# Second attention: queries laid out with tokens over partitions, normalized tile by tile and turned by DMA

## The reference

```python
q = (hidden_states @ q_proj_w.T).reshape(B, Q, NUM_HEADS, HEAD_DIM).transpose(0, 2, 1, 3)   # 32 heads of 128
k = (cross_attention_states @ k_proj_w.T).reshape(B, KV, NUM_KV_HEADS, HEAD_DIM).transpose(0, 2, 1, 3)  # 8 heads
v = ...
q = rmsnorm(q, q_norm_w)          # x * rsqrt(mean(x*x over the 128 of a head) + eps) * w
k = rmsnorm(repeat(k), k_norm_w)
scores = jnp.einsum('bhqd,bhkd->bhqk', q, k) * scale + attention_mask
attn = jax.nn.softmax(scores, axis=-1)
out = jnp.einsum('bhqk,bhkd->bhqd', attn, v)
return out.transpose(0, 2, 1, 3).reshape(B, Q, NUM_HEADS * HEAD_DIM) @ o_proj_w.T
```

## Time and profile before

| what | value |
|---|---|
| median of 3 runs | 2430.42 us (2430.31 to 2433.67) |
| profiled execution, its own time | 2431.65 us |
| its span, first to last instruction | 2429.8 us, granted TensorE clock 0.991 |
| PE busy | 2368.4 us, 97% |
| DVE, ACT, POOL busy | 67%, 52%, 50% |
| second attention, turns 0 to 30 | from 1395.67 us to 2346.45 us of the span |
| DMA, mean | 45 GB/s |

### The profile page before, as it was taken

One profiled execution on the slowest core, in us unless ns is written; L12 is line 12 of the kernel. 1 busy time (PEld: TensorE's weight loads), 2 busy tenths in 40 slices (PEclk: granted clock), 3 DMA queues, 4 the chain that ended last, 5 costly groups with the idle time before them and its releaser, 6 DMA issues.

```text
span 2429.8 us, 45008 instructions
## 1 busy us (share of the span) xinstructions
PE 2368.4 (97%) x17656; PEld 1296.2 (53%) x17664; DVE 1625.0 (67%) x3133; ACT 1253.3 (52%) x2425; POOL 1222.5 (50%) x981
## 2 busy tenths in 40 slices
PE   7899999999999999999999999999999999999998
PEld 4455555555555555444444655555555555555554
DVE  7877777767777788654443566667666666755666
ACT  7665655555555555423232555555555555544453
POOL 3556666666666666223331355444445555445531
PEclk9899999999999999999999999999999999999999
DMA  6111121212121121011100111122121212221101
GB/s 210 45 42 32 51 51 30 53 27 53 27 53 31 42 44 26 29 44 35 44 10 16 40 32 27 42 54 63 36 62 36 62 36 62 53 43 27 27 14 70
DMA packets 216753, 108.13 MB, mean 45 GB/s; under 512 B 169280, under 2 KB 192480, under 8 KB 216544
## 3 DMA queue, kind: packets, MB, share of 16 engines
q1 hardware_dynamic: 216544, 105.25, 17.5%
HBM read 61.62 MB, written 4.19 MB: 27 GB/s over the span
## 4 chain that ended last, share of the span: by engine, by line
PE 61%; POOL 14%; DVE 10%; issue 4%; ACT 4%; POOLq 0%; DVEq 0%; ACTq 0%
PE PB L859 16%; PE PB L811 14%; PE PB L971 9%; PE PB L795 6%; POOL AR L2690 5%; PE PB L988 5%; POOL AR L2695 4%; POOL PSP L2708 3%; PE PB L836 2%; PE PB L901 2%; DVE AR L2116 2%; DVE WB L1921 2%; PE PB L767 1%; POOL AR L2685 1%; ACT JUNK L1321 1%
## 5 line engine op out<-in xcount | busy, mean ns | idle before, releaser
L859 PE MATMUL PB<-WB,AR 128*128 128x512 f16 x3072 | 689.0, 381 | 8.2 <-issue 3.9
L811 PE MATMUL PB<-XTB,WB 128*128 128x512 f16 x3072 | 677.9, 379 | 3.4 <-ACT WB L1357 1.9
L859 PEld LDWEIGHTS PB<-WB,AR 128*128 128x128 f16 x3072 | 298.0, 98 | 368.0 <-issue 15.4
L811 PEld LDWEIGHTS PB<-XTB,WB 128*128 128x128 f16 x3072 | 297.0, 98 | 346.2 <-issue 3.1
L2701 POOL TENSOR_TENSOR AR<-AR,SML 128x512 f32<-128x512 f32 x128 | 144.6, 1151 | 317.0 <-DVE SML L2101 317.0
L2131 DVE SCALAR_TENSOR_TENSOR X<-PB,SML,X 128x512 f32<-128x512 f32 x256 | 189.4, 747 | 168.2 <-PE PB L859 162.0
L1481 ACT ACTIVATE AR<-PB 128x512 f16<-128x512 f32 x256 | 131.5, 596 | 233.1 <-PE PB L901 233.1
L2690 POOL TENSOR_TENSOR AR<-AR,CST 128x512 f32<-128x512 f32 x128 | 182.2, 1423 | 39.6 <-ACT AR L1391 39.6
L2011 DVE TENSOR_TENSOR AR<-PB,AR 128x512 f16<-128x512 f32 x128 | 88.1, 690 | 168.2 <-ACT AR L1444 168.2
L971 PE MATMUL PB<-XTB,AR 128*128 128x512 f16 (+1 forms) x864 | 192.5, 379 | 0.0
L1397 ACT ACTIVATE AR<-AR 128x512 f16<-128x512 f32 x128 | 80.5, 630 | 206.7 <-POOL AR L2695 205.3
(11 more groups left out here) (272 smaller groups left out, 3770.8 us busy)
## 6 DMA issues: line engine op xcount, KB each, us to landing
STG<-in_wo SPq DMA_DIRECT2D x14, 1024.0 KB
STG<-in_wq SPq DMA_DIRECT2D x13, 1024.0 KB
STG<-in_qw_gu SPq DMA_DIRECT2D x40, 128.0 KB
STG<-in_ctxT SPq DMA_DIRECT2D x4, 1024.0 KB
X<-in_x SPq DMA_DIRECT2D x4, 1024.0 KB, 11.1
out_x<-X SPq DMA_DIRECT2D x16, 256.0 KB, 2.4
STG<-in_wk SPq DMA_DIRECT2D x14, 256.0 KB
STG<-in_wv SPq DMA_DIRECT2D x14, 256.0 KB
```

The costliest lines, as they stand in the source:

```text
L811: m = pe.do.matmul(b[:, :], wq[x][:, k, h * 128:(h + 1) * 128], XT[y][c][:, k, :], start=n == 0, stop=n == 11)
L859: m = pe.do.matmul(b[:, :], AT[x][:, h, t * 128:(t + 1) * 128], wo[y][:, h, :], start=n == 0, stop=n == 11)
```

## The change

Only the second attention is touched.

- PE takes each 128-token tile t of the queries as the stationary operand and the weights of all four heads as the moving one: a bank now holds 128 tokens over partitions and 4 heads of 128 along it. There are as many matmuls, of the same size. `norm_q` and `turn_k` on PE are gone.
- For each tile: ACT squares (`squares_1`), DVE sums over each head's 128 and scales (`sums_1`, two instructions), POOL raises 4 columns to -1/2 (`power_1`), DVE multiplies the bank by them (`queries_1`), ACT writes the high half, POOL the low half (DVE for tile 3, `low_1`). The squares and sums of tile t stand ahead of the multiplication of tile t-1.
- SP turns two tiles, both halves, by two DMAs of 64 partitions each (`turn_q`), twice a unit. `scores` waits for the second (`qt_in`).
- Keys of units 0 and 1 are turned by DMA too. Keys and values of unit 2 are made at the end of turn 0 instead of in turn 1.
- In the softmax the multiplication by the norms is gone; the mask is added straight from PSUM.
- Output tiles use banks 4, 5, 2, 3 in turns up to the last but one.

```diff
+        QHP = [words(a, 1024, F16) for a in (10752, 5632)]
+        QHL = [QHP[t // 2][:, 1024 * (t % 2):1024 * (t % 2) + 1024] for t in range(4)]
+        QT_rows = words(0, 2048, F16).rearrange("p (o t n) -> p o t n", o=2, t=4)
...
+            return ((4, 5, 2, 3) if L and u < NU - 2 else (2, 3, 0, 2))[t]
...
+            def turn_q(u, two):
+                for t in (2 * two, 2 * two + 1):
+                    sp.wait_ge(q_hi, (1, u, t))
+                    sp.wait_ge(*halved(u, t))
...
+                for odd in range(2):
+                    sp.do.dma_start_transpose(out=QT_rows[:, odd, 2 * two:2 * two + 2, :].rearrange("p t (a q) -> p (t a) q", a=8),
+                                              in_=QHP[two][64 * odd:64 * odd + 64, :]).then_inc(qt_in.of((u, two), 16), 16)
...
+                    elif u < NU - 1:
+                        turn_p_pair(1, u, 0)
+                        turn_p_pair(1, u, 1)
+                        turn_q(u + 1, 0)
                         turn_k(u + 1)
+                        turn_q(u + 1, 1)
...
+            def queries_1(u, t):
...
+                        m = pe.do.matmul(b[:, :], XT[x][c][:, k, t * 128:(t + 1) * 128], wq[y][:, k, :],
+                                         start=n == 0, stop=n == 11)
...
+                if L:
                     pe.wait_ge(kt_in, u)
+                    pe.wait_ge(qt_in, (u, 1))
...
+                    if (L, u) == (1, 0):
+                        keys_values(2, 0)
+                        keys_values(2, 1)
...
+            def sums_1(u, t):
+                g, rs = UNITS[1][u][0], RSQ[:, 4 * t:4 * t + 4]
+                dve.wait_ge(q_sq, (u, t))
+                dve.do.tensor_reduce(rs, M1[t].rearrange("p (h d) -> p h d", h=4), AX, ALU.add).then_inc(q_sum.of((u, t)), 1)
+                dve.wait_ge(q_sum, (u, t))
+                dve.do.tensor_scalar(rs, rs, 1.0 / DH, eco(1, g, 0), ALU.mult, ALU.add).then_inc(q_ms.of((u, t)), 1)
+
+            def queries_1(u, t):
+                dve.wait_ge(q_pow, (u, t))
+                dve.do.tensor_tensor(M1[t].rearrange("p (h d) -> p h d", h=4), PB[QB[t]][:, :].rearrange("p (h d) -> p h d", h=4),
+                                     RSQ[:, 4 * t:4 * t + 4].unsqueeze(2).to_broadcast([128, 4, DH]), ALU.mult
+                                     ).then_inc(q_mul.of((u, t)), 1)
...
-                    dve.do.tensor_tensor(v[pair], by_batch(PB[4 + pair][:, :]),
-                                         RSQ[:, pair * BC:(pair + 1) * BC].unsqueeze(2).to_broadcast([128, BC, SQ]),
-                                         ALU.mult).then_inc(s_out.of((1, u, pair)), 1)
+                    dve.do.scalar_tensor_tensor(v[pair], by_batch(PB[4 + pair][:, :]), PWN[:, 2:3],
+                                                MASK1.unsqueeze(1).to_broadcast([128, BC, SQ]), ALU.mult, ALU.add
+                                                ).then_inc(s_out.of((1, u, pair)), 1)
...
+                    for t in range(4):
+                        power_1(u, t)
+                        if t > 0:
+                            queries_1(u, t - 1)
+                        if t < 2 and beside > 0:
+                            halved_p(1, beside, t)
+                        if t == 2 and u > 1:
+                            halved_k(u)
+                        side(1, beside, 1 + t)
```

361 lines of the change are left out of this document (170 added, 191 removed).

## The result

| | median of the runs, us | ratio to the kernel before, 95% interval | span, us | clock |
|---|---|---|---|---|
| before | 2430.36 | | 2429.8 | 0.991 |
| changed | 2523.56 (2521.29 to 2526.55) | 1.0381 [1.0369, 1.0393] | 2519.5 | 0.98 |

A forecast was written before the change was run, and what follows sets the result against it. PE, busy 97% of the span, was taken as the bound. From 2431.65 us, entry +9.7 and -0.6, later turns -5.6, -9.6, +2.5, -2.5 gave 2425.5; the runs' median, 1.2 lower, 2424.3; range 2404 to 2449.

The forecast's parts named there:

- PE's floor: PE, second attention: a turn without norm_q's 0.80 us takes 28.93; turns 12 to 15 together 116.5 instead of 118.9.
- Step 1: DVE's weighed, mask and maximum, then the softmax up to POOL's soft_norm: POOL starts at D + 8.41 us.
- D: Start of DVE's weighed, counted from the start of PE's scores: 0.68 us behind a turn with weight work.
- The entry: Turns 0 and 1: 65 us in place of 55.25, +9.7, through added PE idle time; -0.6 ahead of turn 0.
- nothing to 3.4 us for the clock: Turns 0 and 1: the clock behind the idle times costs between nothing and 3.4 us in each.
- step 4: SP issues two query transposes, 1.23 us to issue one, last landing 3.1 after its issue: D + 28.8.
- The rival with slow transposes: SP's last pair ahead of the scores: 2.5 us later, half of it per turn, kernel at 2448; 24%.
- steps 2 and 3: POOL without a gap to tile 3's power, 13.8 us, D + 22.2; then DVE, ACT, DVE to D + 24.3.
- a rival of its own: Path through DVE and POOL longer by 1 to 1.5 us: -0.2 a turn left, kernel at 2430; 24%.
- The loop forgives: PE waiting at scores lets DVE start weighed earlier: a path longer by x costs about x/2 a turn.
- only remove waits that PE doesn't have in plain turns: Output banks and sums-ahead order: worth nothing, covered by the 10.4 us of output tiles.
- 30 turns at -0.80: Rival: the wide cover holds everywhere, turns 0 and 1 come out even, kernel at 2405; 12%.

The follow-up runs named there:

- full-width kernel: Changed kernel with each query tile turned by one 128-partition, 1024-column DMA, tokens interleaved and scores reading every second column, all of the reference computed: 2469.23 us.
- best kernel: Full-width transposes, side work at other slots and reordered turns 0 and 1 together, three pieces a slot later still, against the kernel before: 2424.88 us, ratio 0.9969.
- The slots alone: Side work of turns 2, 4 and 27 to 30 put at other slots, nothing added or left out, against the complete kernel with full-width transposes: 2442.37 us.

## Why the prediction was wrong

**What held.** PE's floor of 28.93 us a turn, from the 0.80 that `norm_q` cost: the full-width and the best kernel run turns of 28.93, and the four turns take 117.5 where I had 116.5. Step 1: POOL starts at D + 8.40 (I had 8.41). The entry: 66.2 for turns 0 and 1 against 65, with PE idle for 8.8 us in turn 0 and 11.5 in turn 1, and a mean clock of 0.83 and 0.86. The nothing to 3.4 us for the clock in each of these turns came from no row; behind the 8.8 us wait of turn 0 `weigh` and the keys and values took 1.8 more than at full clock (2.75 and 5.94 against 1.48 and 5.41).

**The step that failed: step 4 and its price.** I took the lower bound for the 64-partition transposes "since bytes and pieces are alike". The price goes by columns more than by bytes. They took 1.74 to issue and 4.3 to land, and the keys' transpose between them 1.81 to issue (median), where it took 1.29 among full-width ones. From tile 3's low half to the scores it is 6.7 us (1842.41 to 1849.08), where I had 4.5 (28.8 less 24.3). In the full-width kernel the same stretch is 3.6 to 4.8 in turns 5 to 22, and PE waits at the scores in 7 turns for 7.1 us, where it waited in 22 for 54.8. The run with one full-width DMA a tile keeps the number of DMAs and the bytes of each and is 56.5 us faster, and the one with two tiles to a DMA, in the old order on SP, keeps 48 of that: it is the shape. The rival with slow transposes named the place and, at 2.5 us, the size; I gave it 24%.

The Trainium skill had spoken against them (SBUF — State Buffer, "Door 1: The DMA port swizzle"), and its direction was right: a DMA of 128 partitions by 2048 columns moved twice the bytes of the 64-partition one in the same 4.3 us. At 1024 columns the gap is smaller: 3.2 us for the full width, 2.7 for half of it. The prediction's estimate from that page's ratio had the pair 1.7 us later, less than the 2.2 measured.

**Mis-sized: steps 2 and 3.** They took 17.3 us (D + 8.4 to D + 25.7) instead of 15.9, 1.1 of the difference in POOL's hand-overs. DVE's scaling of the sums does end with POOL's instruction, as I had it (1829.39 and 1829.37 for tile 0), but POOL's power starts 0.08 behind it and is not free. I had bounded this path at no gap at all and given the 1 to 1.5 us to a rival of its own; both rivals came true at once. Together the path was longer by 3.6. "The loop forgives" held in turns at full clock: D fell from 0.68 to -0.95, and a path of D + 32.4 gave turns of 31.3 and not 33. But the halving starts from 29.2, where a path of D + 28.8 and PE meet (half of 28.93 + 28.8 + 0.68), so 3.6 comes to 31.0; the rival, at turns of 30.1, was too small also by that. By the same working a turn is back at 29.73 with x near 1.1, and not 1.9. And the half clock behind the repeated waits, which I had put into the first two turns only, is 1.7 us in every second or third turn. It keeps the loop from forgiving there, since the exponentials stand behind the copy of the keys and values (9.07 us from the scores to POOL's start, 7.45 at full clock), and with the exponentials ahead the keys' sums come late instead.

**Left out: the tail, and waits that DVE's order makes.** I booked turns 26 to 30 at -0.5 each, because the memory block gives PE 35 us. Turns 26 and 27 took 1.8 and 3.2 more, turns 28 to 30 some 6 each. Turn 25, booked at -0.7, took 6.1 more: PE waits 4.05 for the transposes at its start and 3.35 for the bank of query tile 2, which `tail_setup` wants (L1038). `t_norm` and `t_lg` on DVE and PE follow the query tiles, and these now stand behind POOL's powers, and hold their banks until DVE has multiplied. The slots alone gave 26.9 us at full width, 18 of it in turns 27 to 30. In the same way the prediction's sentence that the output banks and the order "only remove waits that PE doesn't have in plain turns" was wrong for the banks: with the old ones PE would have had such waits, worth 25 us at full width and 6 in the changed kernel, where the wait at the scores hides most of them. For the order it was nearly right, at 0.16 a turn.

**Sums that don't add.** Three rivals are priced off their own terms: 30 turns at -0.80 from 2430.4 are 2406 (2405 in the text); 28 turns at -0.2 with the entry's +9.1 are 2434 (2430); 28 turns at +0.4 with an entry of +12 are 2454 before any half clock (2448), which already lies above my range of 2404 to 2449. None of it reaches 2523.

**What stays open.** The table of shapes holds for these transposes as they stand in this queue; none was timed by itself, so how much of an issue is waiting for the one before it can't be told. Why the clock falls behind some of the 2.3 us waits and not behind the others was not tried (their length doesn't decide it, see below), nor was a change of the interleaved form that keeps the output banks old and moves `peak` to another bank.

## What to carry to other kernels

Price a DMA transpose by its columns as well as by its bytes: here two over half the partitions cost about twice one over all to issue (7.0 against 3.8 us a turn, 10.1 against 4.9), and where two halves must come apart, interleave them in the partitions and read with a stride. When work moves onto a path through four engines, list what is queued behind each new wait and whose PSUM banks are held longer; here that was over a quarter of the loss, and slot numbers were enough to mend it. Where two rivals lengthen the same path, work out their sum too.
